# A gated delta recurrence on one core: the fourth gate tile of a chunk moves from block 0 to block 5

## What is computed

```python
def step(S, xs):
    q_t, k_t, v_t, a_t, b_t = xs
    Sk = jnp.einsum('bhvk,bhk->bhv', S, k_t)
    S = a_t[..., None] * S - (b_t[..., None] * (Sk - v_t))[..., None] * k_t[:, :, None, :]
    o_t = jnp.einsum('bhvk,bhk->bhv', S, q_t)
    return (S, o_t)
...
_, o = lax.scan(step, S0, (tfirst(q), tfirst(k), tfirst(v), tfirst(a), tfirst(beta)))
...
g = jax.nn.sigmoid(x @ Wg.T).reshape(B_, T_, H, DV)
o = (o * g).reshape(B_, T_, H * DV)
return o @ Wo.T
```

## Time and profile before

| | us |
|---|---|
| median of 3 runs (2405.32 to 2416.09) | 2413.17 |
| the profiled execution | 2418.26 |
| its span, first to last instruction | 2416.5 |
| recurrence: chunks 0 to 11, first L1455 to that of chunk 12 | 1108.56 |
| chunks 12 to 14 | 269.54 |

### The profile page before, as it was taken

One profiled execution on the slowest core, in us unless ns is written; L12 is line 12 of the kernel. 1 busy time (PEld: TensorE's weight loads), 2 busy tenths in 40 slices (PEclk: granted clock), 3 DMA queues, 4 the chain that ended last, 5 costly groups with the idle time before them and its releaser, 6 DMA issues.

```text
span 2416.5 us, 61545 instructions
## 1 busy us (share of the span) xinstructions
PE 2105.1 (87%) x21890; PEld 1602.9 (66%) x21890; DVE 1895.8 (78%) x4382; ACT 1238.9 (51%) x2692; POOL 521.8 (22%) x577
## 2 busy tenths in 40 slices
PE   6999999999995888887888887888888888866999
PEld 4444888888874766775766766667667667753566
DVE  4222799999995888987978978888988988987776
ACT  3000587787782555654645645555555545533332
POOL 0000144444442211211121221121221211222000
PEclk9999999999996888988888888988988888877999
DMA  7000177777779556555556655556566555566540
GB/s 262 9 9 9 62 260 264 268 268 264 266 266 336 200 184 209 208 198 201 202 186 214 207 193 200 197 191 221 195 199 213 180 179 200 193 210 260 199 157 18
DMA packets 229473, 468.45 MB, mean 194 GB/s; under 512 B 48432, under 2 KB 172328, under 8 KB 199640
## 3 DMA queue, kind: packets, MB, share of 16 engines
q1 hardware_dynamic: 226184, 454.06, 53.9%
q10 hardware_dynamic: 2976, 10.72, 1.2%
q0 software_dynamic: 48, 0.16, 0.0%
HBM read 316.36 MB, written 149.57 MB: 193 GB/s over the span
## 4 chain that ended last, share of the span: by engine, by line
PE 45%; DVE 28%; issue 16%; ACT 5%; DMA 4%; DVEq 1%; POOL 1%; ACTq 1%; SPq 0%; POOLq 0%
DVE arena L1066 10%; PE PS L1503 7%; PE PS L1662 5%; PE PS L1517 4%; PE PS L1489 3%; PE PS L1372 3%; PE PS L1581 3%; PE PS L1542 3%; DVE arena L1157 3%; DVE arena L1172 3%; DVE arena L1165 2%; PE PS L1445 2%; PE PS L1395 2%; DVE arena L1149 2%; PE PS L1530 2%
## 5 line engine op out<-in xcount | busy, mean ns | idle before, releaser
L1395 PE MATMUL PS<-arena 128*128 x2048 | 463.7, 387 | 1.8 <-DVEq L1051 1.0
L1066 DVE SCALAR_TENSOR_TENSOR arena<-PS,SM,arena 128x256 f32<-128x256 f32 x1152 | 452.9, 478 | 15.5 <-ACT arena L721 15.5
L1395 PEld LDWEIGHTS PS<-arena 128*128 128x128 f32 x2048 | 383.8, 188 | 81.7 <-DVE arena L1066 6.5
L1503 PE MATMUL PS<-arena 128*128 128x128 f32 x1920 | 321.8, 318 | 38.4 <-ACT arena L860 36.7
L1503 PEld LDWEIGHTS PS<-arena 128*128 128x128 f32 x1920 | 271.5, 219 | 77.9 <-ACT arena L860 55.6
L627 POOL TENSOR_TENSOR arena<-arena 128x256 f32<-128x256 f32 x128 | 114.9, 897 | 914.2 <-DVE arena L1172 914.2
L852 ACT ACTIVATE arena<-arena 128x128 f32<-128x128 f32 x960 | 306.7, 395 | 0.0
L721 ACT ACTIVATE arena<-PS,SM 128x256 f32<-128x256 f32 x384 | 209.5, 564 | 89.3 <-PE PS L1395 84.3
L1111 DVE TENSOR_TENSOR arena<-arena,PS 128x512 f32<-128x512 f32 x192 | 127.5, 685 | 116.5 <-PE PS L1542 112.5
L1489 PE MATMUL PS<-ident,arena 128*128 128x128 f32 x960 | 180.4, 320 | 27.2 <-ACT arena L852 26.1
L1517 PE MATMUL PS<-arena 32*128 32x128 f32 x1920 | 173.5, 330 | 25.7 <-DVE arena L1100 18.0
(11 more groups left out here) (135 smaller groups left out, 3212.5 us busy)
## 6 DMA issues: line engine op xcount, KB each, us to landing
arena<-g_d SPq DMA_DIRECT2D x126, 1024.0 KB, 5.6
arena<-vas_d SPq DMA_DIRECT2D x124, 384.0 KB, 3.2
vas_d<-arena SPq DMA_DIRECT2D x32, 1024.0 KB, 11.4
kq_d<-arena SPq DMA_DIRECT2D x8, 4096.0 KB, 11.5
arena<-kq_d SPq DMA_DIRECT2D x14, 2048.0 KB, 7.9
arena<-beta_d SPq DMA_DIRECT2D x8, 2048.0 KB, 9.2
kb_d<-arena SPq DMA_DIRECT2D x8, 2048.0 KB, 10.3
vas_d<-arena SPq DMA_DIRECT2D x8, 2048.0 KB, 12.4
```

Of the source, the lines that this page charges most:

```text
L1066: nc.vector.scalar_tensor_tensor(acc, raw[:, :, i:i + PT_], CW[:, w, i, hh:hh + 1], acc, ALU.mult, ALU.add).then_inc(job_free if i == TAPS ...
L1395: ins = mm(dst.rearrange("p (b n) -> p b n", b=B), W4[:, w, kt, DH * h:DH * (h + 1)], XNT[:, kt, :, bass.ds(c * PT_ + (HALO - halo), halo ...
L1503: ins = mm(bank(7)[:, 128 * gi:128 * (gi + 1)].rearrange("v (l x) -> v l x", l=NB), STR[:, s % 2, gi, :], KQ[d][:, :, p0:p0 + 2].rearrange ...
```

## The change

Of the four gate tiles of an early chunk, three stay in block 0, now those of heads 0, 2 and 3; head 1's goes to the end of block 5, behind the key transposes and ahead of `corr_transposes(5)`. Its sigmoid stands on ScalarE at the end of block 5, ahead of `corr_copy(5)`; its store, and the loads of WGA and XG that may only follow its matmuls, stand on SyncE in block 6. The load of WGB is issued by ScalarE at the chunk's start and waits for the first half of `carried` only.

```diff
+GATE_HEAD = [0, 2, 3, 1]
+GATE_BANK = [6, 7, 6, 6]
...
                 if early:
-                    it, q = early
-                    sp.wait_ge(corr_full, n * 9 + 2)
-                    sp.dma_start(WGB, wg_v[:, :, DH * (4 * q + 2):DH * (4 * q + 4)]).then_inc(wgb_in, 16)
-                    for k in range(4):
-                        sp.wait_ge(early_gate, n * 4 + k + 1)
...
-                        if k == 1:
-                            load_wga((q + 1) % 4)
-                    if q == 3:
-                        load_xg(it * -128 + (128 * (NCH - 2) + HALO))
+                    for k in range(3):
+                        store_gate(k)
...
+                    if m == 6 and early:
+                        store_gate(3)
+                        load_wga((early[1] + 1) % 4)
+                        if early[1] == 3:
+                            load_xg(early[0] * -128 + (128 * (NCH - 2) + HALO))
...
                     if m == 0 and early:
-                        for k in range(4):
-                            act.wait_ge(early_psum, n * 4 + k + 1)
+                        q = early[1]
+                        act.wait_ge(corr_full, n * 9 + 1)
+                        act.dma_start(WGB, wg_v[:, :, DH * (4 * q + 2):DH * (4 * q + 4)]).then_inc(wgb_in, 16)
+                        for k in range(3):
                             if k == 2:
                                 act.wait_ge(r_stored, n * 128 + 64)
-                            nc.scalar.activation(GST[k], bank(6 + k % 2), ACT.Sigmoid).then_inc(early_gate, 1)
+                            gate_tile(k)
...
+                    if m == 5 and early:
+                        act.wait_ge(r_stored, n * 128 + 192)
+                        gate_tile(3)
                     if m < NB - 1 or nxt:
                         corr_copy(m)
...
+                    if s == 11 and early:
+                        pe.wait_ge(early_gate, n * 4 + 4)
...
                     if m == 0 and early:
-                        early_gates()
+                        for g in range(3):
+                            early_gate_tile(g)
...
+                    if m == 5 and early:
+                        early_gate_tile(3)
                     if m < NB - 1 or nxt:
                         corr_transposes(m)
```

More of the change, by code:

```diff
@@ L301, in build @@
         x_v = x_tm.rearrange("(n p) d -> p n d", p=128)
+        wg_v = wgT.rearrange("(c p) n -> p c n", p=128)
         def silu_of(x):
@@ L437, in _ @@
             sp.wait_ge(xnT_stored, 16)
-            wg_v = wgT.rearrange("(c p) n -> p c n", p=128)
             xn_v = xnT_d.rearrange("p (k b n) -> p k b n", k=2, b=B)
@@ L1494, in reads_of @@
                     pe.wait_ge(tr_ready, n * 16 + s + 1)
+                    if s == 0 and early:
+                        pe.wait_ge(early_gate, n * 4 + 2)
                     if s == 0:
                         pe.wait_ge(kq_in[d], (i + 1 + c) * 16)
-                        if early:
-                            pe.wait_ge(early_gate, n * 4 + 4)
                     else:
@@ L1566, in prep_taken, with early_gate_tile @@
                             pe.wait_ge(pd_done, d_item(n, x))
-                def early_gates():
-                    for k in range(4):
-                        if k == 0:
-                            pe.wait_ge(xg_in, early[0] * 16 + 16)
-                            pe.wait_ge(wga_in, n * 16 + 16)
-                        else:
-                            if k == 2:
-                                pe.wait_ge(wgb_in, n * 16 + 16)
-                            if k >= 2:
-                                pe.wait_ge(early_gate, n * 4 + k - 1)
-                        w = (WGA, WGB)[k // 2]
-                        for kt in range(2):
-                            ins = mm(bank(6 + k % 2), w[:, kt, DH * (k % 2):DH * (k % 2 + 1)], XG[:, kt, :], start=(kt == 0), stop=(kt == 1))
-                        ins.then_inc(early_psum, 1)
+                def early_gate_tile(k):
+                    if k == 0:
+                        pe.wait_ge(xg_in, early[0] * 16 + 16)
+                        pe.wait_ge(wga_in, n * 16 + 16)
+                    elif k == 1:
+                        pe.wait_ge(wgb_in, n * 16 + 16)
+                    elif k == 2:
+                        pe.wait_ge(early_gate, n * 4 + 1)
+                    w, h = (WGA, WGB)[k in (1, 2)], GATE_HEAD[k] % 2
+                    for kt in range(2):
+                        ins = mm(bank(GATE_BANK[k]), w[:, kt, DH * h:DH * (h + 1)], XG[:, kt, :], start=(kt == 0), stop=(kt == 1))
+                    ins.then_inc(early_psum, 1)
                 def keep_awake(count):
```

14 lines of the change are left out of this document (11 added, 3 removed).

## The result

The changed kernel takes 2376.35 us (median of 4 runs, 2373.53 to 2392.70) where the one before takes 2414.63 (4 runs, 2405.32 to 2429.84) beside it: the ratio is 0.9873, 95% interval 0.9846 to 0.9901, so some 31 us less (24 to 37); the two medians themselves lie 38 us apart. The profiled execution took 2377.0 us against 2418.26 before.

The account below looks back on a forecast made before the run. No engine is full, so the waits of each stage decide, with block 0's end set by TensorE. The terms -19.7 - 9.1 + 1 give -28 us, so 2385 us against the 2413.2 median; range 2360 to 2409.

Parts of the forecast that it names:

- part 1: Block 0: one gate tile fewer in twelve chunks, 1.64 us each, 19.7 us gained.
- part 2: Block 0: WGB load issued earlier, by ScalarE, removes 9.1 us of weight waits; at worst 2.3 us wait a chunk.
- part 3: End of block 5: added tile mostly covered by idle time and the key mask wait; cost 1 us, bounds 0 to 3.6.
- clock in blocks 0 and 1: Rival: changed chunks fall to the lower clock there, losing 2 us each, 24 in all, 2409 us; chance 0.15.
- clock in block 6: Rival: filled idle time in block 5 holds the higher clock, 1.5 us a chunk, 18 us more gained, 2367 us; chance 0.22.
- that an earlier L1530 shortens the chunk: Block 0's first correction transposes: starting at 14.75 instead of 16.38 us went with chunks of 89.20 instead of 91.16.
- rival with a tile at 1.2 GHz: Rival: block 5's tile runs at the lower clock on the path, 3.42 us a chunk, 41 in all, 2425 us; chance 0.04.
- Part 4: Block 6: SyncE's moved store and loads fit into its existing wait of 4.9 us; cost nil.

Follow-up runs that it names:

- e1_load: Kernel before with only the WGB load moved to ScalarE, all four gate tiles left in block 0: 2399.59 us, ratio 0.9951 to the kernel before.
- e4_notile5: Changed kernel without the fourth gate tile's matmuls and sigmoid in block 5: 2391.42 us, ratio 0.9922 to the kernel before.
- e3_fill5: Kernel before plus two filler matmuls, result unread, at the end of block 5: 2403.07 us, ratio 0.9986 to the kernel before.
- e10_load_fill: Kernel before with the WGB load on ScalarE and two filler matmuls in block 5, four tiles in block 0: 2379.02 us, ratio 0.9886 to the kernel before.
- e8_behind: Changed kernel with block 5's tile behind the level transposes, its sigmoid behind the copy: 2394.53 us, ratio 0.9913 to the kernel before.
- e11_fill2: Changed kernel plus one useless matmul at the end of block 2: 2382.87 us, ratio 0.9887 to the kernel before.
- e6_keys: Changed kernel with chunk 1's three key loads issued by SyncE ahead of the loop instead of by ScalarE: 2376.88 us, ratio 0.9855 to the kernel before.

## Why the prediction was right, and where it was not

Forecast and traces, in us for the whole kernel; measured is the difference of the table's rows times 11, and chunk 0 apart:

| step of the prediction | forecast | measured |
|---|---|---|
| parts 1 and 2, block 0 of chunks 1 to 11 | -27 | -30 |
| the same in chunk 0 | -1.6 | +8.4 |
| part 3, tile in block 5 (4 to 5) | +1 | +11 (+4 at VectorE) |
| clock in blocks 0 and 1 (a rival, up to +24) | 0 | +6 |
| clock in block 6 (a rival, -18) | 0 | -30 (-24 at VectorE) |

The second figure counts from one level subtraction of VectorE to the next (L1111 and L1126) instead of the transposes.

The 2376.35 us lie in the range and near the 2385 forecast, but through errors of both signs; that they nearly cancel is luck. The cost of the new tile and of chunk 0 came out too small, and the clock in block 6, which paid for both, stood in the sum at nothing. Of the three signs that the prediction named for being wrong two appeared: a wait for wgT ahead of the second tile (in chunk 0), and slow reads in blocks 0 and 1 (in seven chunks). The third, a level subtraction of block 5 over 1 us later, did not: 0.6 us at most. (Chunk 0's later blocks, -5, and the small changes of the other steps make up the rest of the 42.5 us.)

*Parts 1 and 2 in block 0* went as worked out: transposes near 13.2 (12.97 to 13.03 in seven chunks), VectorE's wait gone in these, no wait for weights in chunks 1 to 11. e1_load confirms the size of part 2 in these chunks, 9.7 us. For part 1 the step that failed is a claim, not a number: "that an earlier L1530 shortens the chunk", read from chunks 2 and 3. From e1_load to e4_notile5 the transposes come 1.51 us sooner and 1.30 of it goes into the lower clock behind them; what is left at the end of the chunk, the runs do not settle. The rival "the clock takes it back" was dismissed because no idle time of 2.06 us would arise; the slow reads came in 7 of 12 chunks without such a gap.

*Chunk 0* was misread in part 2. The prediction put the longest landing, 9.7 us, aside: it "belongs to a load behind others on SyncE's queue, and this one is first on its own". The trace of the kernel before has it the other way round. The 9.7 us are chunk 0's, from a queue of SyncE's with nothing else under way, amid ScalarE's start-up loads; and on ScalarE's queue the load of chunk 0 is not first but stands behind eight others. It left 1.6 us later than before, not sooner, and landed after 15.5 us. That was the one wait of TensorE for these weights, 6.83 us, where the bound had been 2.3.

*Part 3* failed in its size. The cover (the wait for the key mask) was real, and in chunk 3 it held to 0.14 us. But it was read from chunk 1 of the kernel before, where TensorE reached this place 1.55 us early. In seven of eleven chunks of the changed kernel a slow read ahead makes it late, and the tile delays the corrections by 1.1 us each, of which VectorE waits 0.4 to 0.6: 4 us in all, just above the bound of 3.6 (the rest of the 11 in the table comes off the next step). The rival with a tile at 1.2 GHz didn't happen: the tile took 1.88 us each time.

*Block 6.* The rival "block 6 at full clock" had 0.22 and was, with block 0, one of the two large gains. That added work holds the clock is confirmed by three runs: without the tile (e4_notile5) the lower clock returns in 11 chunks, with useless work in its place (e3_fill5, e10_load_fill) it goes in 8 and 10. That the idle time ahead of the transposes is what makes it drop is not: in seven of those 11 chunks there was 0 to 0.3 us of it, and e8_behind holds the clock with the tile behind the transposes. Its price was too low: 1.5 us per chunk, from two operations on TensorE, where VectorE's step to this block shrank by 2.14 (its wait by 2.44 from chunk 1 before to chunk 2 after) and that of the transposes by 2.74. Part 3's cost and this gain belong to the same tile; from block 4 to 6 they leave -1.78 per chunk, 20 us. The prediction held the two in separate cases when they come together.

*Part 4* was right: SyncE's move shows nowhere.

**What stays open.** Why the clock falls behind block 0 when a tile less stands there, and in some chunks in blocks 4 and 5, isn't settled. Chunks 2 and 3 of the changed kernel have the same work and the same idle times in block 0 up to 15.9 us after the carried product; the state update there is fast in the one and slow in the other. Timeline, chunk 2 and then chunk 3:

```profile
961.86 1.16 PE L1534 MATMUL PS<-arena 32*128 32x128 f32 x16
...
1046.77 1.86 PE L1534 MATMUL PS<-arena 32*128 32x128 f32 x16
1048.56 2.08 PE L1520 MATMUL PS<-arena 128*128 128x128 f32 x8
```

So idle time alone does not tell when the clock falls; the same is seen in e4_notile5 and e8_behind. e11_fill2 moved such stretches and removed none. And whether e4_notile5 is truly slower than the changed kernel rests on the blocks' steps and the counts; the intervals of the times overlap (0.9894 to 0.9949 against 0.985 to 0.9937). Nor is it shown what the tile less in block 0 is worth by itself, nor what chunk 0 would take with its weights on SyncE and all else as changed.

## What to carry to other kernels

Where TensorE changes between its two clocks, price an edit by the clock of what follows, and not only by its own length: added work can cost nothing or less, and work taken out can lose most of its length again right behind the place. When a load moves to another engine's queue, look at the first pass through the loop apart from the others, and at what that queue still has under way there. And when a cover is read from one chunk, read it in chunks with the lower clock too before it is counted for all.

## What the runs showed of the hardware

- TensorE's granted clock decides more here than its work. The same state read of eight records takes 2.08 us at 1.2 GHz and 1.16 at 2.4 GHz, and the stretch around a slow one makes the step from block 0 to 1 of the changed kernel 9.8 to 11.4 us long instead of 8.42. The mean granted clock of the runs is no guide to the time: 0.926 for e3_fill5 at 2403 us, 0.907 for e4_notile5 at 2391, 0.922 for the changed kernel at 2376.
- The clock can be held by matmuls whose result nobody reads: two of 128 x 512 in block 5 took the slow reads of block 6 from 8 chunks to 2 (e1_load to e10_load_fill). They need not stand in the idle time itself: with the tile behind the transposes (e8_behind) none of 12 is slow.
- How long 256 KB take to land depends on what is under way and on the queue: 2.7 us at the least; amid start-up loads that move some 410 GB/s, 9.7 to 11.1 us from SyncE's queue with nothing else on it (three kernels) and 15.5 to 17.2 from ScalarE's behind five to eight loads (nine kernels). Which engine issues the large loads made no difference (16.2 in e6_keys).
